# Index preparation of a graph kernel: moves computed after the ranking, masks in two five-lane instructions, four row batches in the scatter ring

## The reference, cut to what matters

```python
edge_index = jnp.stack([src, dst])
x = _layernorm(x + _L0_gnn_ref(x, edge_index, ...))     # three layers, each:
#   neigh_mean = segment_sum(h[dst], src) * inv_deg
#   out = elu(h @ Wg + deg_pos * (neigh_mean @ Wl + h @ Ws) + b)
x = _layernorm(x + _L1_gnn_ref(x, edge_index_t, edge_attr_64, edge_attr_64_n2, edge_attr_64_n3, ...))
#   per edge: [x[src], stf] and [x[dst], ef, et], summed over src, then W1, relu, W2
```

## Time and profile before

| | |
|---|---|
| time, median of 3 runs | 12008.17 us (12000.91 to 12014.21) |
| span of the profiled execution | 12006.2 us |
| PE busy | 7020.0 us (58%) |
| DVE busy | 6572.9 us (55%) |
| POOL busy | 5053.8 us (42%) |
| ACT busy | 3664.2 us (31%) |
| DMA | 2320.70 MB, mean 193 GB/s |

### The profile page before, as it was taken

How to read it: one execution, slowest core, us unless ns; L and a number is a source line. 1 busy time by engine, 2 the same in 40 slices (tenths; PEclk the granted TensorE clock), 3 DMA queues, 4 the chain that set the end, 5 groups by cost and what they waited for, 6 DMA issues and landing times.

```text
span 12006.2 us, 213561 instructions
## 1 busy us (share of the span) xinstructions
PE 7020.0 (58%) x46640; PEld 6056.7 (50%) x46640; DVE 6572.9 (55%) x19818; ACT 3664.2 (31%) x10935; POOL 5053.8 (42%) x4833
## 2 busy tenths in 40 slices
PE   7999998000049997545565555555536555655556
PEld 6898886000038886444344444444434444444445
DVE  8459998000046665444675456655567555665546
ACT  0003332000037775333571115811139211571111
POOL 0018888666644444554015550055500455215550
PEclk9999999999999998666797777977769777897776
DMA  9905555565569997455495564955629655885560
GB/s 385 366 20 144 145 144 142 137 148 137 144 194 304 301 301 225 142 142 135 165 346 161 164 164 155 358 164 163 160 52 395 201 163 160 269 333 161 164 161 18
DMA packets 1567398, 2320.70 MB, mean 193 GB/s; under 512 B 974516, under 2 KB 1046056, under 8 KB 1567320
## 3 DMA queue, kind: packets, MB, share of 16 engines
q1 hardware_dynamic: 1227608, 1356.73, 33.5%
q0 software_dynamic: 292608, 911.36, 27.5%
q10 hardware_dynamic: 47104, 51.75, 1.8%
HBM read 1328.55 MB, written 986.78 MB: 193 GB/s over the span
## 4 chain that ended last, share of the span: by engine, by line
PE 28%; issue 25%; DVE 19%; another core or an unknown queue 13%; ACT 7%; DVEq 4%; DMA 3%; ACTq 1%; POOL 0%; SPq 0%; POOLq 0%
PE ps L750 10%; PE ps L818 5%; PE ps L703 4%; DVE mask L1319 3%; DVE oh_s L1350 3%; ACT ring L1059 3%; DMA gathered<-ring 2%; PE ps L738 2%; ACT hring L1069 2%; PE ps L743 2%; DVE prod L1303 2%; PE ps L787 2%; DVEq L362 1%; DVE ohj L1209 1%
## 5 line engine op out<-in xcount | busy, mean ns | idle before, releaser
L641 POOL DMA_INDIRECT ring<-gathered,gidx x2176 | 2089.5, 960 | 3930.5 <-DMA gathered<-ring 2098.6
L571 POOL DMA_INDIRECT by_src<-prow,ppos x1562 | 1924.9, 1232 | 1485.5 <-DMA ppos<-pos 940.6
L818 PE MATMUL ps<-ring,oh_s 128*128 128x192 bf16 x8704 | 1217.8, 294 | 1797.3 <-DVE oh_s L1350 1585.3
L1354 DVE TENSOR_REDUCE red<-ps 128x64 f32<-128x192 f32 x2720 | 957.1, 352 | 2351.2 <-remote 1285.1
L818 PEld LDWEIGHTS ps<-ring,oh_s 128*128 128x128 bf16 x8704 | 918.6, 127 | 2059.2 <-DVE oh_s L1350 961.0
L1083 ACT CAST hring<-foh 128x512 f32<-128x512 bf16 x544 | 361.2, 664 | 3585.7 <-DVE foh L1350 3065.2
L1432 DVE CAST ring<-ps 128x384 bf16<-128x384 f32 x2176 | 1126.8, 553 | 328.1 <-PE ps L743 274.1
L743 PE MATMUL ps<-hring,oht_g 128*128 128x192 bf16 x8704 | 941.8, 246 | 544.7 <-DVE ring L1432 150.1
L750 PE MATMUL ps<-frows,hring 128*128 128x193 f32 x4352 | 1182.6, 433 | 4.2 <-issue 3.9
L1059 ACT CAST ring<-ps 128x384 bf16<-128x384 f32 x2176 | 1138.4, 524 | 10.1 <-PE ps L743 9.8
L1350 DVE TENSOR_TENSOR oh_s<-loc,iota_loc 128x512 bf16<-128x512 bf16 x2720 | 1126.5, 414 | 5.3 <-ACT loc L1027 3.1
(11 more groups left out here) (217 smaller groups left out, 12841.3 us busy)
## 6 DMA issues: line engine op xcount, KB each, us to landing
gathered<-ring SPq DMA_DIRECT2D x544, 768.0 KB
by_src<-zeros SPq DMA_DIRECT2D x34, 6272.0 KB, 45.5
frows<-by_src SPq DMA_DIRECT2D x544, 392.0 KB
oht_g<-oht SPq DMA_DIRECT2D x544, 256.0 KB, 5.4
gathered<-got SPq DMA_DIRECT2D x136, 776.0 KB
prow<-in_edge_attr_n SPq DMA_DIRECT2D x284, 352.0 KB
bc<-tidrow ACTq DMA_DIRECT2D x313, 160.0 KB
prow<-in_edge_attr SPq DMA_DIRECT2D x142, 352.0 KB
```

What stands on the lines that cost most here:

```text
L571: pool.indirect_dma_start(out=table, out_offset=bass.IndirectOffsetOnAxis(ap=ppos[:, s, j:j + 1], axis=0), in_=prow[:, s, j, :], in_offset ...
L641: pool.indirect_dma_start(out=ring[:, c, :], out_offset=None, in_=gb, in_offset=offsets(g, c % 4)).then_inc(q.got[c], 16)
L818: mm = pe.matmul(ps[:, c % 4, 0:HW], oh_s[:, c % 4, :, k], ring[:, c, k * HW:(k + 1) * HW], start=k == 0, stop=k == K - 1)
L1354: return dve.tensor_reduce(red[:, u], ps[:, bank, 0:HW].rearrange("p (a d) -> p d a", d=D), AX.X, ALU.add)
```

## The change

It does four things.

1. The moves stand behind the ranking, on DVE and PE. All their instructions are the same as before.
2. In a ranking step the five `scalar_tensor_tensor` instructions of 128 elements that made the mask (equal, then times the upper triangle) are two `tensor_tensor` instructions of 640 elements: one compares `bc` with `tid["s"]`, broadcast along the 128 elements of a lane, at the start of the step; one multiplies by `upper_bf`, broadcast over the lanes, at its end. A semaphore `s_same` lies between them.
3. The ring of the scatter has 4 batches. SP therefore waits for the positions in groups of `AHEAD` = 9 steps (was 7) and loads four batches ahead of the first scatter.
4. The three layers share one set of semaphores with an offset `c0` for each layer in place of a set for each.

```diff
+RING = 4
+USES = PBATCHES // RING
...
-        prow = sb_early("prow", [P, 3, PB, ROW])
-        ppos = sb_early("ppos", [P, 3, PB], I32)
+        prow = sb_early("prow", [P, RING, PB, ROW])
+        ppos = sb_early("ppos", [P, RING, PB], I32)
...
-            AHEAD = -(-3 * PB // LANES)
+            AHEAD = -(-RING * PB // LANES)
             sp.wait_ge(s_meta, 1)
-            for s in range(3):
+            for s in range(RING):
                 load(s, 0, True)
             sp.wait_ge(s_pos, AHEAD)
-            for s in range(3):
+            for s in range(RING):
                 places(s, 0)
...
             pool.wait_ge(s_clear, 16 * (3 + NB // CLEAR))
-            for s in range(3):
+            for s in range(RING):
                 scatter(s, 0)
...
-            for k in (1, 2):
-                def moves(j, u):
-                    pe.wait_ge(s_cmp, j + (1 + (k - 1) * NG))
...
             rank(STEPS - 1, 0, False)
+            for k in (1, 2):
+                def moves(j, u):
+                    pe.wait_ge(s_cmp, j + (1 + (k - 1) * NG))
...
-            dve.wait_ge(s_prep_v, 6)
+            def select(n, u):
...
+            def rank(m, u, first):
+                n, v = 6 * m + u, u % 3
+                if not first:
+                    dve.wait_ge(s_t, n - 2)
+                dve.wait_ge(s_bc[v], 32 * m + (u // 3 * 16 + 16))
+                u = v
+                dve.tensor_tensor(mask[:, u], bc[:, u, :].rearrange("p (l q) -> p l q", q=P),
+                                  tid["s"][:, bass.ds(n * LANES, LANES)].unsqueeze(2).to_broadcast([P, LANES, P]),
+                                  ALU.is_equal).then_inc(s_same, 1)
+                bins_of(ohi[:, u], "s", n)
+                bins_of(ohj[:, u], "d", n)
+                dve.tensor_scalar(oht_e[0:T, u, :], bc[0:T, u, :], iota_part[0:T, 0:1], None, ALU.is_equal)
+                dve.wait_ge(s_same, n + 1)
+                dve.tensor_tensor(mask[:, u], mask[:, u], upper_bf[:, :].unsqueeze(1).to_broadcast([P, LANES, P]),
+                                  ALU.mult).then_inc(s_roh, 1)
...
-                bins_of(ohi[:, u], "s", n)
-                bins_of(ohj[:, u], "d", n)
-                dve.tensor_scalar(oht_e[0:T, u, :], bc[0:T, u, :], iota_part[0:T, 0:1], None, ALU.is_equal)
-                for l in range(LANES):
-                    ins = dve.scalar_tensor_tensor(mask[:, u, l, :], bc[:, u, l * P:(l + 1) * P],
-                                                   tid_f[:, bass.ds(n * LANES + l, 1)], upper_bf[:, :],
-                                                   ALU.is_equal, ALU.mult)
-                ins.then_inc(s_roh, 1)
...
-                    dve.wait_ge(q.mm, i + 1)
-                    if not isinstance(i, int) or i > 1:
-                        dve.wait_ge(q.parts, i - 1)
+                    dve.wait_ge(q.mm, i + (q.c0 + 1))
+                    if q.c0 > 0 or not isinstance(i, int) or i > 1:
+                        dve.wait_ge(q.parts, i + (q.c0 - 1))
```

More of the change, by code:

```diff
@@ L240, in build @@
         s_mv = sem("s_mv")
-        s_plod = [sem(f"s_plod{u}") for u in range(3)]
-        s_pout = [sem(f"s_pout{u}") for u in range(3)]
+        s_plod = [sem(f"s_plod{u}") for u in range(RING)]
+        s_pout = [sem(f"s_pout{u}") for u in range(RING)]
         s_prest = sem("s_prest")
@@ L575, in _ @@
             pool.wait_ge(s_clear, 16 * (3 + NB // CLEAR))
-            for s in range(3):
+            for s in range(RING):
                 scatter(s, 0)
-            with pool.Fori(1, TAIL_PB) as i:
-                for s in range(3):
+            with pool.Fori(1, USES) as i:
+                for s in range(RING):
                     scatter(s, i)
-            scatter(0, TAIL_PB)
+            for s in range(2):
+                scatter(s, USES)
             pool.wait_ge(s_prest, 80)
@@ L584, in _ @@
             pool.indirect_dma_start(
[L585 to L586 removed]
+                out=table, out_offset=bass.IndirectOffsetOnAxis(ap=ppos[0:REST, 2, 0:1], axis=0),
+                in_=prow[0:REST, 2, 0, :], in_offset=None).then_inc(s_prout, 16)
             def offsets(g, c):
@@ L697, in _ @@
                 mm.then_inc(s_prep_t, 1)
-            for k in (1, 2):
-                def moves(j, u):
-                    pe.wait_ge(s_cmp, j + (1 + (k - 1) * NG))
-                    for c in range(4):
-                        mm = pe.matmul(flat[:, bass.ds(j * 4 + (1024 * (k + 1) + c), 1)], cmp[0:T + 1, u, c, :],
-                                       steps[k][0:T + 1, bass.ds(j * 4 + c, 1)], start=True, stop=True)
-                    mm.then_inc(s_mv, 1)
-                with pe.Fori(0, NG // 8) as m:
-                    for u in range(8):
-                        moves(8 * m + u, u % 2)
             def rank(n, u, first):
@@ L732, in _ @@
             rank(STEPS - 1, 0, False)
+            for k in (1, 2):
+                def moves(j, u):
+                    pe.wait_ge(s_cmp, j + (1 + (k - 1) * NG))
+                    for c in range(4):
+                        mm = pe.matmul(flat[:, bass.ds(j * 4 + (1024 * (k + 1) + c), 1)], cmp[0:T + 1, u, c, :],
+                                       steps[k][0:T + 1, bass.ds(j * 4 + c, 1)], start=True, stop=True)
+                    mm.then_inc(s_mv, 1)
+                with pe.Fori(0, NG // 8) as m:
+                    for u in range(8):
+                        moves(8 * m + u, u % 2)
             def turned(q, b, u, bank, one_hots):
@@ L1269, in _ @@
                 dve.memset(cmp[:, 0, 0, 0:1], 0.0).then_inc(s_prep_v, 1)
-            dve.wait_ge(s_prep_v, 6)
+            def select(n, u):
+                v, u = u % 3, u % 2
+                dve.wait_ge(s_t, n + 1)
+                dve.tensor_tensor(prod[:, u], ps[:, 1 + v, 0:LANES * T].rearrange("p (l b) -> p l b", b=T),
+                                  ohj[:, v].rearrange("p b l -> p l b"), ALU.mult).then_inc(s_sel, 1)
+                dve.wait_ge(s_sel, n + 1)
+                with nc.allow_low_precision(reason="one whole number below 2**24 in a row of zeros"):
+                    dve.tensor_reduce(pos[:, bass.ds(n * LANES, LANES)], prod[:, u], AX.X, ALU.add).then_inc(s_pos, 1)
+            def rank(m, u, first):
[13 more added lines that the diff above has]
+                                  ALU.mult).then_inc(s_roh, 1)
+            for u in range(6):
+                rank(0, u, u < 3)
+                if u > 1:
+                    select(u - 2, u - 2)
+            with dve.Fori(1, STEPS // 6) as m:
+                for u in range(6):
+                    rank(m, u, False)
+                    select(6 * m + (u - 2), (u - 2) % 6)
+            rank(STEPS // 6, 0, False)
+            for n in range(STEPS - 3, STEPS):
+                select(n, n % 6)
             for k in (1, 2):
@@ L1298, in _ @@
                     rows_of_gb(move[1], iota_row_i[:, :], movef[:, :])
[L1300 to L1336 removed]
+            for s in range(RING):
+                dve.wait_ge(s_pout[s], (USES + (1 if s < 2 else 0)) * (PB * 16))
             dve.wait_ge(s_prout, 16)
```

123 lines of the change are left out of this document (49 added, 74 removed).

## The result

The changed kernel takes **12469.56 us** (median of 4 runs, 12460.1 to 12474.72), the kernel before on the same chip 12005.17 us. The ratio is 1.038, interval 1.037 to 1.040: slower, where 11370 us and faster had been forecast.

What follows compares the result with a forecast made beforehand. POOL's scatter, ending at 3413 us, was taken as the bound. Start at 632, 695 columns at 1.35 us and 867 at 1.39 end it at 2775, 638 us less: 11370 us, range 11240 to 11560.

Steps and rivals of the forecast that it cites:

- Start at 632 us: With the moves behind the ranking, the first scatter column starts at about 632 us in place of 862, 230 us earlier.
- Mask durations 0.83 and 0.56 us: In a ranking step on DVE, the first new mask takes 0.83 us and the second 0.56 us.
- The new masks don't stop POOL: Beside the ranking, the 1.4 us per step for which the old masks stopped POOL's scatter go.
- A step is then 3.8 to 3.9 us: The ranking takes 313 x 3.85 = about 1205 us, ends near 1570, and isn't on the chain.
- hidden until the scatter would end before 2040: Moves on PE and DVE, some 1570 to 2040 us, lie under the scatter, whose floor ends at 2600 us.
- 1.35 us a column beside the ranking: POOL's scatter pace from 632 to 1570 us, giving 695 columns; bounds 1.29 and 1.96 us.
- Moves' `cmp` free for POOL: Behind the ranking, the moves' `cmp` is a `tensor_tensor`, the kind that POOL was not stopped by.
- Ring: a third to a half of 154 us: A fourth batch saves a third to a half of POOL's 154 us of waits for loads behind the ranking.
- Rival 4: SP's issue stays slow for the whole scatter; at 21.5 us a batch it ends at 3685, 12280 us; chance 0.03.

Runs made afterwards that it cites:

- e11: The changed kernel itself, unchanged, on a chip of the second kind: 10064.32 us, ratio 0.960 to the kernel before.
- e3: The kernel before with the ring of four alone, on a chip of the second kind: 10494.92 us, ratio 1.000.
- e1: The kernel before with the two new mask instructions alone, on a chip of the second kind: 10181.65 us, ratio 0.970.
- e15: The changed kernel with five scatter paces one after the other beside the ranking, on a chip of the first kind: 12153.33 us, ratio 1.013.
- e18: The changed kernel with a 128x256 GpSimd memset ahead of each column in the first 22 of 35 ring rounds, first kind: 11687.84 us, ratio 0.971.
- e7: The changed kernel with 12 empty GpSimd instructions behind each scatter column, on a chip of the first kind: 12330.79 us, ratio 1.028.

## Why the prediction was wrong

- *Start at 632 us*: right (640.9; 640.0 in e11).
- *Mask durations 0.83 and 0.56 us*: 0.821 and 0.483. *The new masks don't stop POOL*: right in that no column of 2.3 to 2.5 us is left (the longest is 1.62 us, the median 961 ns). But they aren't free: on the second kind, where the ranking goes at full pace, a column beside it takes 753.95/674 = 1.12 us in the mean, and up to 1.58 when it starts just behind the first mask. The prediction had misread its own row there: the short column (1200.83 to 1201.79) lies beside the reduce, `ohi` and the start of `ohj`, not beside `prod`, which had ended at 1200.30.

```profile
L1296 DVE TENSOR_TENSOR mask<-bc,tid_s 128x640 bf16<-128x640 bf16 x313 | 256.8, 821 | 53.0 <-DMA bc<-tidrow 38.7 <-issue 9.3 <-PE ps L723 1.4
...
L1303 DVE TENSOR_TENSOR mask<-mask,upper_bf 128x640 bf16<-128x640 bf16 x313 | 151.2, 483 | 0.0
```

- *"A step is then 3.8 to 3.9 us and the ranking ... about 1205 us, ending near 1570. That alone is worth nothing, for the ranking is not on the chain"*: **this is the step that failed.** It took the ranking's length as independent of the scatter. It was 2965 us (357 to 3322), since beside a free scatter ACT waited up to 12.1 us for one of PE's signals, of which a step needs five one after the other, and so the ranking became what the scatter waits for: 628 us more of waits for positions (708 against 80) take back 221 us of start and all that the masks' stops had cost.
- *Moves "hidden until the scatter would end before 2040"*: failed as a consequence: they end at 3858, and their exposed part is the measured loss.
- *1.35 us a column beside the ranking*: 1.42 on the second kind (959/674, the missing 0.07 beside masks and `ohi`) and 2749/1542 = 1.78 on the first, starving included. *Moves' `cmp` free for POOL*: wrong, 1.64 us a column in e11; the evidence for it was `ohi`, which is bf16, while `cmp` is fp32.
- *Ring: a third to a half of 154 us*: not seen. e3 has ratio 1.000, and e1, with the ring of three, hardly waited for loads there either (863.0 us in 12 waits, 859.7 of them ahead of the first column). On the first kind it can't be read, since waits for positions cover it.
- *Rival 4 (slower)* had the right side and the nearest evidence: SP's issues took 0.71 us where POOL ran free and 0.38 behind a stop of POOL (8.1 us, ahead of its column at 2415). But it put this down to SP alone and asked only whether SP could keep up with POOL; that the ranking could be slowed had no rival at all. In the preparation nothing on PE, DVE or ACT stood beside a free scatter, so none of the rows gave the price of 10 us. The trace of the kernel before had it nevertheless, in the main part, where POOL gathers by indirect DMA 1.25 us apart; the prediction didn't look there. DVE's waits there (of the same line in e3, on the second kind, none is for "remote"):

```profile
DVE red L1354 <- remote: 1285.1, 348, 18.8
```

- The forecast was for one chip of the first kind. On a chip of the second kind the same sum gives 436 us (2831 for e3's 3267) and ratio 0.960; the share forecast was 0.947.

What stays open is why PE's signals are late and those to PE aren't, which resource the scatter fills on chips of the first kind (the writing of descriptors, the memory that they lie in, or the way of the semaphores), and why only there.

## What to carry to other kernels

A wait or a stop can protect someone: before taking away what slows an engine that writes DMA descriptors, look in the trace at how the others' signals do where that engine already runs free (here SP's issues in the tail, and DVE's waits for PE in the main part), and price everything that will newly stand beside it. Work moved "under" such a stream is hidden only if its own signals get through. Time a change on more than one chip: this one is worth +3.8% or -4.0% by the chip alone, and with a small pause (0.2 to 0.3 us a column, for 968 of the 1562 columns) it is worth -2.9% and -2.7% on the two kinds: the pause rescues the first and costs 1.3 points on the second.

## What the hardware showed that I had not expected

- Two kinds of Trainium2 chips under one program: 10492 to 10521 us and 11986 to 12033 us for the kernel before.
- On the slower kind, indirect DMAs issued every 1.27 us by GpSimd delay TensorE's signals to ScalarE from 0.45 us to 9 to 12 us, with a first 2.7 us after 20 us and the full delay after some 70 (e15); ScalarE's and VectorE's signals to TensorE stay at 0.05 to 0.17 us. At 1.6 us a column the longest such wait is 4.1 us (e18), at 1.9 us it is 0.8 (e15).
- Empty instructions of GpSimd between indirect DMAs cost nothing (e7), a memset of 128x256 with its own semaphore costs 0.20 us (1.46 for 1.26 us a column).
- A column of the scatter that starts just behind a 99x512 fp32 `tensor_tensor` of VectorE takes 1.40 us in place of 0.96 (e11).
